# Image patches loaded and turned by token tile, text and image tiles alternating

## The reference

```python
patches = patchify(images, 16)                       # [32, 36, 768]
h_img = einsum('bnd,ed->bne', patches, W_proj) + b_proj + pos_emb
h_txt = take(weights, positions(x_txt), axis=0)      # [32, 32, 256]
h = concatenate([h_img, h_txt], axis=1)              # [32, 68, 256]
h = h + attn(layernorm(h))    # projections dt, x, gate; convolution; state-space scan; output
h = h + ffn(layernorm(h))     # top 2 of 4 experts
```

## Time and profile before

| | us |
|---|---|
| median of 3 runs | 496.74 (496.46 to 499.77) |
| span of the profiled execution | 495.2 |
| its mean granted clock of TensorE | 0.967 |
| TensorE busy | 442.5 (89%) |
| VectorE busy | 330.5 (67%) |
| ScalarE busy | 296.4 (60%) |
| GpSimd busy | 152.2 (31%) |
| stage A, until the first dt projection | 63.7 |

### The profile page before, as it was taken

How to read it: one execution, slowest core, us unless ns; L and a number is a source line. 1 busy time by engine, 2 the same in 40 slices (tenths; PEclk the granted TensorE clock), 3 DMA queues, 4 the chain that set the end, 5 groups by cost and what they waited for, 6 DMA issues and landing times.

```text
span 495.2 us, 9980 instructions
## 1 busy us (share of the span) xinstructions
PE 442.5 (89%) x3149; PEld 363.4 (73%) x3149; DVE 330.5 (67%) x980; ACT 296.4 (60%) x667; POOL 152.2 (31%) x255
## 2 busy tenths in 40 slices
PE   8989989799899999999999798999999999999400
PEld 5769967667778878887777577888878888888300
DVE  6885567678999434335786777866674666666584
ACT  2854359177975465316554354887786777877341
POOL 2000000000000000001243887874778644543322
PEclk9999999799999999999999999999999999999955
DMA  7981089900019942972511222232322333252262
GB/s 178 187 228 56 33 253 322 292 0 2 1 35 259 217 114 58 228 228 81 180 54 52 89 94 77 86 97 66 107 98 76 107 107 110 74 155 69 78 213 82
DMA packets 58734, 59.94 MB, mean 121 GB/s; under 512 B 25368, under 2 KB 51260, under 8 KB 57404
## 3 DMA queue, kind: packets, MB, share of 16 engines
q1 hardware_dynamic: 54236, 48.68, 36.4%
q0 software_dynamic: 3552, 9.74, 5.3%
q10 hardware_dynamic: 896, 0.89, 0.6%
HBM read 34.50 MB, written 24.80 MB: 120 GB/s over the span
## 4 chain that ended last, share of the span: by engine, by line
PE 66%; DVE 12%; issue 7%; ACT 7%; POOL 4%; DMA 2%; SPq 1%; DVEq 0%; POOLq 0%; ACTq 0%
PE bank L1040 14%; PE bank L881 9%; PE bank L433 8%; PE bank L435 8%; PE bank L434 8%; PE bank L955 3%; PE bank L1030 3%; PE bank L901 3%; POOL sorted_x L671 2%; PE bank L1012 2%; ACT U L470 1%; DVE spj L1400 1%; DMA got<-expert_y 1%; PE bank L848 1%; PE bank L947 1%
## 5 line engine op out<-in xcount | busy, mean ns | idle before, releaser
L1040 PE MATMUL bank<-w,hr 128*128 x320 | 76.0, 380 | 1.5 <-DVE ysb L1661 1.5
L1040 PEld LDWEIGHTS bank<-w,hr 128*128 128x128 f32 x320 | 60.1, 190 | 11.7 <-issue 2.7
L644 POOL MEMSET ones<- 2x128 f32 x1 | 0.2, 194 | 212.3 <-PE bank L916 212.3
L1234 ACT ACTIVATE hr<-bank,gsel 128x128 f32<-128x128 f32 x160 | 59.9, 460 | 0.2 <-PE bank L1030 0.2
L719 POOL DMA_INDIRECT expert_y<-ysb,toid x40 | 42.8, 1071 | 51.3 <-DVE ysb L1661 34.7
L881 PE MATMUL bank<-Tb,U 68*32 68x68 f32 x1024 | 45.9, 358 | 0.3 <-issue 0.3
L881 PEld LDWEIGHTS bank<-Tb,U 68*32 68x32 f32 x1024 | 40.6, 139 | 3.6 <-issue 3.1
L1646 DVE BATCH_NORM_STATS2 bsth<-bank 128x6 f32<-128x512 f32 x40 | 27.7, 693 | 20.5 <-PE bank L435 20.2
L671 POOL DMA_INDIRECT sorted_x<-x2s,slot x34 | 33.8, 994 | 15.3 <-issue 9.2
L1226 ACT ACTIVATE hn<-bank,nmrh,rsh 128x512 f32<-128x512 f32 x40 | 31.1, 777 | 10.0 <-DVE nmrh L1655 8.1
L433 PE MATMUL bank<-w_hi,bT_hi 128*128 x80 | 35.0, 438 | 0.1
(11 more groups left out here) (297 smaller groups left out, 1153.3 us busy)
## 6 DMA issues: line engine op xcount, KB each, us to landing
Tb<-ssm_kernels SPq DMA_DIRECT2D x16, 680.0 KB, 7.5
sorted_x<-zpad SPq DMA_DIRECT2D x6, 1419.0 KB, 13.6
xg<-sorted_x SPq DMA_DIRECT2D x40, 129.0 KB, 2.1
got<-expert_y SPq DMA_DIRECT2D x17, 256.0 KB, 3.6
XI<-in_x_dram SPq DMA_DIRECT2D x12, 288.0 KB, 5.6
h0r<-h_spill SPq DMA_DIRECT2D x17, 128.0 KB, 2.1
out_dram<-acc SPq DMA_DIRECT2D x17, 128.0 KB
w1raw<-in_L_ffn_w_dram SPq DMA_DIRECT2D x4, 512.0 KB, 15.9
```

The costliest lines, as they stand in the source:

```text
L1040: mm = pe.matmul(bank[6][:, 0:D], hr[:, i % 3, c, :], w2[:, bass.ds(expert[i], 1), c, :].rearrange("p o n -> p (o n)"), start=(c == 0), st ...
L1234: last = act.activation(hr[:, i % 3, c, :], bank[3 + i % 2][:, c * P:(c + 1) * P], ACT.Relu, scale=gsel[:, i, 0, c:c + 1], bias=gsel[:, i, ...
```

## The change

The images are loaded by token: for each of the 36 positions one load of 32 partitions (the batch) with the 16 pieces of 192 bytes, into the rows of its tile in XI. Four loads make a tile, so all patches of a tile can be turned in two ring steps of three 128x128 transposes, 18 steps in all in place of 24, and an image tile waits only for its own two. Landings are counted in groups: tile 0, tiles 1 and 2, 3 and 4, 5 and 6, 7 and 8. TILE_ORDER alternates text and image tiles and ends with image tile 8. Two img steps stand in every second step, one image tile ahead; vec moves from the ring's start to step 4, and the six weight steps to steps 5, 7, 9, 11, 15 and 16. The filling matmul before each img step is gone. SP issues tok, tabl, the 36 image loads and only then vec_rows. The stores of h0 are in groups of four tiles in the order of their making, and the reading of h0 back follows that. BLOCK_ORDER becomes [0, 3, 4, 1, 2]. The number of bytes moved and the arithmetic of each tile are the same.

The diff, cut to its core:

```diff
@@ -248,7 +246,7 @@
 
 
         x = ins["x"]
-        img = x.rearrange("(g b) (hp py) w c -> g (b hp) py (w c)", g=2, py=PS)
+        img = x.rearrange("b (hp py) (wp px) c -> hp wp b py (px c)", py=PS, px=PS)
         w_dram = [ins[n].rearrange("(c p) d -> p c d", p=P) for n in ("L0_attn_W_dt", "L0_attn_W_x", "L0_attn_W_g")]
 
         def rows(name):
@@ -275,32 +273,43 @@
 
 
 
-        TILE_ORDER = list(range(NTI, NT)) + list(range(NTI))
-        BLOCK_ORDER = [3, 4, 0, 1, 2]
-
-        H0_OUT = [(0, NH0), (NH0, NH0 + 3), (NH0 + 3, NH0 + 6), (NH0 + 6, NT)]
+        TILE_ORDER = [t for n in range(NH0) for t in (NTI + n, n)] + [NTI - 1]
+        BLOCK_ORDER = [0, 3, 4, 1, 2]
+
+        H0_OUT = [(m, min(m + NH0 // 2, NT)) for m in range(0, NT, NH0 // 2)]
 
         def ready_tiles(nb):
 
             t0, t1 = BLOCKS[nb][0] // P, (BLOCKS[nb][0] + BLOCKS[nb][1]) // P
             return 1 + max(TILE_ORDER.index(t) for t in range(t0, t1))
 
-        PREP = [("pos", 0), ("pos", 1), ("vec",)] + [("wp", c) for c in range(0, CK, 2)]
-        IMAGES = [("img", half, g, wp) for g in range(2) for wp in range(HP) for half in range(2)]
+        PREP = [("pos", 0), ("pos", 1)] + [("wp", c) for c in range(0, CK, 2)]
         WEIGHTS = [("w", w, dc) for w in range(3) for dc in range(DC)]
-        A_RING = PREP + IMAGES + WEIGHTS
-        LAST_IMAGES = (len(PREP) + len(IMAGES) - 2, len(PREP) + len(IMAGES) - 1)
-
-        A_STEPS = [("ring", q) for q in range(len(PREP))]
-        ahead = list(range(len(PREP), len(A_RING)))
+        image = lambda i: [("img", i, half) for half in range(2)]
+
+
+        A_RING = PREP + image(0)
+        A_STEPS = [("ring", q) for q in range(len(A_RING))]
+
+        def ring(steps):
+            for step in steps:
+                A_STEPS.append(("ring", len(A_RING)))
+                A_RING.append(step)
+
+        WEIGHTS_AT = [5, 7, 9, 11, 15, 16]
         for k in range(NT + 3):
             A_STEPS += [(f"a{s + 1}", TILE_ORDER[k - s]) for s in (3, 2, 1, 0) if 0 <= k - s < NT]
-            count = 3 if k < NH0 else 1
-            A_STEPS += [("ring", q) for q in ahead[:count]]
-            ahead = ahead[count:]
+            if k % 2 == 0 and k // 2 + 1 < NTI:
+                ring(image(k // 2 + 1))
+            if k == 4:
+                ring([("vec",)])
+            if k in WEIGHTS_AT:
+                ring([WEIGHTS[WEIGHTS_AT.index(k)]])
             if k in (NT, NT + 1):
                 A_STEPS.append(("dt", k - NT))
-        assert not ahead
+        assert all(step in A_RING for step in WEIGHTS + image(NTI - 1))
+        landing = lambda i: (i + 1) // 2
+        images_to = lambda q: sum(step[0] == "img" for step in A_RING[:q + 1])
 
 
         FB = [list(range(i, min(i + 2, NT))) for i in range(0, NT, 2)]
@@ -426,7 +435,7 @@
         def h0_out(eng):
 
             for n in range(len(H0_OUT)):
-                eng.wait_ge(sem(f"h0_stored{n}"), 32 if n == len(H0_OUT) - 1 else 16)
+                eng.wait_ge(sem(f"h0_stored{n}"), 16)
 
         def split3(pe, out_ap, a_hi, a_lo, b_hi, b_lo, start, stop):
 
@@ -443,18 +452,17 @@
             act.activation(spt[:, q % 4, 0:w], spt[:, q % 4, 0:w], ACT.Ln, bias=onec[:]).then_inc(sem("dt_ln"), 1)
 
         def patches(ps):
-            return ps[:, 0:KT * ROWS].rearrange("p (k b hp) -> p k hp b", k=KT, hp=HP)
-
-        def patches_hi(half, g, wp):
-            return pT_hi[:].rearrange("p c (hp wp) b -> p c hp wp b", wp=HP)[
-                :, half * KT:(half + 1) * KT, :, wp, g * GB:(g + 1) * GB]
+            return ps[:, 0:KT * P].rearrange("p (k n) -> p k n", k=KT)
+
+        def patches_hi(i, half):
+            return pT_hi[:].rearrange("p c t b -> p c (t b)")[:, half * KT:(half + 1) * KT, i * P:(i + 1) * P]
 
         def lo_chunk(c):
             return pT_lo[0][:, c, 0:LI * B] if c < KT else pT_lo1[:, c - KT].rearrange("p t b -> p (t b)")
 
-        def patches_lo(half, g, wp):
+        def patches_lo(i, half):
             a = pT_lo[0][:, 0:KT, 0:LI * B] if half == 0 else pT_lo1[:].rearrange("p c t b -> p c (t b)")
-            return a.rearrange("p c (hp wp b) -> p c hp wp b", hp=HP, wp=HP)[:, :, :, wp, g * GB:(g + 1) * GB]
+            return a[:, :, i * P:(i + 1) * P]
 
         def turned(eng, step, who):
 
@@ -477,33 +485,25 @@
         @block.sync
         def _(sp):
             sp.dma_start(tok[:], ins["x_txt"]).then_inc(sem("tok_in"), 16)
+            sp.dma_start(tabl[:], ins["L0_txt_weights"][0:LT + 2, :]).then_inc(sem("table_in"), 16)
+            for i in range(NTI):
+                for n in range(TPT):
+                    t = TPT * i + n
+                    sp.dma_start(XI[n * B:(n + 1) * B, i].rearrange("b (y k) -> b y k", k=PWC),
+                                 img[t // HP, t % HP]).then_inc(sem(f"img_in{landing(i)}"), 16)
             at_row = 0
             for n in VECS:
                 a = rows(n)
                 sp.dma_start(vec_rows[at_row:at_row + a.shape[0], :], a).then_inc(sem("vecs_in"), 16)
                 at_row += a.shape[0]
-            sp.dma_start(tabl[:], ins["L0_txt_weights"][0:LT + 2, :]).then_inc(sem("table_in"), 16)
-            for g in range(2):
-                for wp in range(HP):
-                    sp.dma_start(XI[:, g, wp].rearrange("p (y k) -> p y k", k=PWC),
-                                 img[g][:, :, wp * PWC:(wp + 1) * PWC]).then_inc(sem(f"img_in{g}{wp // 2}"), 16)
             for w in range(3):
                 sp.dma_start(Wr[w][:], w_dram[w]).then_inc(sem(f"w_in{w}"), 16)
 
             for n, (m0, m1) in enumerate(H0_OUT):
                 sp.wait_ge(sem("h0_copied"), m1)
-                t0 = TILE_ORDER[m0]
-                if m0 % NH0 + m1 - m0 <= NH0:
-                    sp.dma_start(h0d[t0:t0 + m1 - m0].rearrange("t p d -> p t d"),
-                                 h0s[:, m0 % NH0:m0 % NH0 + m1 - m0, :]).then_inc(sem(f"h0_stored{n}"), 16)
-                else:
-
-                    cut = NH0 - m0 % NH0
-                    sp.dma_start(h0d[t0:t0 + cut].rearrange("t p d -> p t d"),
-                                 h0s[:, m0 % NH0:, :]).then_inc(sem(f"h0_stored{n}"), 16)
-                    sp.dma_start(h0d[t0 + cut:t0 + m1 - m0].rearrange("t p d -> p t d"),
-                                 h0s[:, 0:m1 - m0 - cut, :]).then_inc(sem(f"h0_stored{n}"), 16)
-                if n == 0:
+                sp.dma_start(h0d[m0:m1].rearrange("m p d -> p m d"),
+                             h0s[:, m0 % NH0:m0 % NH0 + m1 - m0, :]).then_inc(sem(f"h0_stored{n}"), 16)
+                if n == 1:
                     for k in range(2):
                         sp.dma_start(bcs[:, k], state(("L0_attn_B_ssm", "L0_attn_C_ssm")[k])).then_inc(sem("small_in"), 16)
                     sp.dma_start(cw[:], ins["L0_attn_conv_w"].rearrange("(c p) o k -> p c (o k)", p=P)).then_inc(sem("small_in"), 16)
@@ -557,7 +557,7 @@
                 if kind == "h0in":
                     if i >= 4:
                         sp.wait_ge(sem("h1"), i - 3)
-                    sp.dma_start(h0r[:, i % 4, :], h0d[i]).then_inc(sem(f"h0_back{i % 4}"), 16)
+                    sp.dma_start(h0r[:, i % 4, :], h0d[TILE_ORDER.index(i)]).then_inc(sem(f"h0_back{i % 4}"), 16)
                     if i == 3:
                         for t, name in ((ong_b, "L0_ffn_on_g"), (onb_b, "L0_ffn_on_b")):
                             sp.dma_start(t[:], ins[name].partition_broadcast(P)).then_inc(sem("w2_in"), 16)
@@ -755,8 +755,6 @@
                     ps = bank[q % 4]
                     if kind == "wp":
                         warm(ps, 2)
-                    elif kind == "img":
-                        warm(ps, 1)
                     if kind == "vec":
                         pe.wait_ge(sem("vecs_in"), 16 * len(VECS))
                         mm = pe.transpose(ps[:, 0:NV], vec_rows[0:NV, :], ident[0:NV, 0:NV])
@@ -779,12 +777,11 @@
                         for j in range(HC):
                             mm = pe.transpose(ps[:, j * P:(j + 1) * P], Wr[w][:, j, dc * P:(dc + 1) * P], ident[:])
                     else:
-                        half, g, wp = rest
-                        pe.wait_ge(sem(f"img_in{g}{wp // 2}"), 32)
+                        i, half = rest
+                        pe.wait_ge(sem(f"img_in{landing(i)}"), 16 * TPT * min(2, landing(i) + 1))
                         for kk in range(KT):
                             c0 = (half * KT + kk) * P
-                            mm = pe.transpose(ps[:, kk * ROWS:(kk + 1) * ROWS], XI[:, g, wp, c0:c0 + P],
-                                              ident[0:ROWS, 0:ROWS])
+                            mm = pe.transpose(ps[:, kk * P:(kk + 1) * P], XI[:, i, c0:c0 + P], ident[:])
                     mm.then_inc(sem("a_ps"), 1)
                 elif step[0] == "a1":
                     i = step[1]
@@ -800,7 +797,7 @@
                         mm = pe.matmul(ps, at_i, tabl_lo[:], start=False, stop=True)
                     else:
```

(14 more changed lines are left out.)

2 lines of the change are left out of this document (1 added, 1 removed).

## The result

| | before | after |
|---|---|---|
| median of the runs, us | 497.53 (495.67 to 500.0, 8 runs) | 501.5 (499.69 to 503.24, 8 runs) |
| ratio of the times, 95% interval | 1 | 1.0081 (1.0059 to 1.0102) |
| span of the profiled execution, us | 495.2 | 498.0 (its time 499.69) |
| mean granted clock there | 0.967 | 0.962 (other runs 0.953 to 0.959) |

What follows compares the result with a forecast made beforehand. VectorE was taken to bound 12 to 34 us and TensorE 34 to 63; mixing them gains 3.0, less 0.6 at the stage's end, 0.5 for vectors and 0 for blocks: 1.9, so 494.8 us, range 489.5 to 501.

Steps and rivals of the forecast that it cites:

- The start: First ring steps: first image tile at 14.0 us, step 3 at 19.4 and not 17.9.
- The step of the table load: ScalarE, behind the copy of tile 0: loading the square-root table takes 1.28 us; TensorE stands still 1.5 before step 3.
- The loads: SP's queue: 36 image loads at 0.5 us make 18; vectors land at 24.5, making TensorE wait about 0.5 in step 4.
- upper bound: Image loads: 0.14 us per boundary between loads, 5 us for 36; vectors come at 27.5, a wait of 3.7.
- rival 3: Image loads late, vectors and first weights at 27.5 or later, clock perhaps lost: 3 to 5 us, 498.5; 13%.
- The wait inside a pair: Text steps wait for VectorE's xs: 1.97 us, 2.64 after weights; image steps 2.95 or 3.39; pairs 4.92 or 6.03.
- rival 1: Text and image pairs: VectorE reaches xs sooner, pairs take TensorE's own 4.40 and 4.84 us, giving 489.5; 15%.
- The 0.6 given back by the late weight step: End of the image stage: last weight step in step 16, so later xs come 2.64 us after the start, not 1.97.
- The block order: dt projections: q = 8 at 97.6 us, q = 12 at 103.1; between 0.7 gained and 0.6 lost, taken as 0.
- rival 2: Text steps without filling matmuls: clock falls to 1.2 GHz, some 2.2 us a fall; repeated falls 10%, one (497) 12%.
- the price list: Clock falls at image tiles between 17 and 60 us: some 2.2 us each, three falls make 501.4.
- the 1.6 us that I had called safe: Patch and image stage: no expected standstill over 1.6 us, less than half the 3.65 idle in which the clock fell.

Runs made afterwards that it cites:

- g3: e4 with ScalarE's square-root table loaded early, behind the patch copies of step 0: 497.91 us, ratio 1.0001 to the kernel before.
- e2: Changed kernel with the eight vector loads behind the twelve image loads of tiles 0 to 2: 501.38 us, ratio 1.0077 to the kernel before.
- e3: Changed kernel with the old block order (3, 4, 0, 1, 2): 500.13 us, ratio 1.0057 to the kernel before.
- e4: Changed kernel with the vector loads first and the old block order: 497.41 us, ratio 0.9994 to the kernel before.
- e1: Changed kernel with the eight vector loads ahead of the 36 image loads again: 498.75 us, ratio 1.0021 to the kernel before.
- g2: e4 with weight steps in 7, 9, 11, 13, 15 and 16, none in step 5: 496.52 us, ratio 0.9976 to the kernel before.
- g4: Changed kernel with the 18 filling matmuls put back ahead of the patch steps: 501.55 us, ratio 1.0096 to the kernel before.
- j2: Changed kernel with 35 instead of 20 filling matmuls, ahead of dt projection q = 4: 506.05 us, ratio 1.0147 to the kernel before.
- k1: Changed kernel with 13 filling matmuls directly ahead of dt projection q = 8: 503.09 us, ratio 1.0100 to the kernel before.
- g1: e4 with the 18 filling matmuls put back ahead of the patch steps: 497.66 us, ratio 1.0011 to the kernel before.
- h1: g2 and g3 together (vectors first, old block order, weights from step 7, early table): 494.24 us, ratio 0.9944 to the kernel before.
- h2: h1 with the 18 filling matmuls ahead of the patch steps: 494.71 us, ratio 0.9944 to the kernel before.
- j1: Changed kernel with eleven filling matmuls in step 4 ahead of the wait for the vectors: 501.0 us, ratio 1.0059 to the kernel before.
- k2: h1 with 15 filling matmuls directly ahead of dt projection q = 8: 490.74 us, ratio 0.9856 to the kernel before.
- j4: h1 with 35 filling matmuls ahead of dt projection q = 4: 496.94 us, ratio 0.9984 to the kernel before.
- i1: Kernel before with its 12 image loads cut into 36 of 32 partitions each: 503.75 us, ratio 1.0118 to the uncut kernel.

## Why the prediction was wrong

The sum went from -1.9 to +2.8 on the profiles, and to 4.0 in the medians. Term by term:

- **The start: right chain, missed load.** Step 3 came at 20.86, expected 19.4. The images were put 2.8 us earlier "beside the patch weights on ScalarE's queue", whose transfer I priced, but not the small loads behind it there: bpb and araw now come late, and VectorE is 1.2 us behind. Vectors first gives 0.4 to 0.8 of it back. The step of the table load was right: with the table early, step 3 comes 1.5 us sooner (g3). The late start isn't a loss of its own, though. Step 4 waited for the vectors in any case; with step 3 on time it would have waited 4.1 us and not 2.6 (an estimate from their landing at 28.0).
- **The loads: this step failed.** "I take 0.5: 36 x 0.5 = 18": they took 21.97 us. Of the 4.0 that were missing, 35 loads at 0.54 make 1.4, and the one load of 3.11 makes 2.6. For running "beside the patch weights on ScalarE's queue" I had put nothing into the value that I took, only into its bounds. Where the start is as before, a load takes 0.55 to 0.59 on average. The vectors came at 28.0, beyond even my upper bound of 27.5, whose 0.14 a boundary was close to the 0.12 measured; I had dropped it for the nearer-looking 0.50 of a weight load. The wait was 2.61 us, not 0.5. (The 0.5 doesn't follow from my own times either: vectors at 24.5 and TensorE at 23.8 make 0.7.) I had named this as rival 3 (3 to 5 us, 498.5, 13%) with "the idle TensorE may lose the clock too". And I priced vectors and weights apart, where they are one queue: e2 shows that a cure for the one is paid at the other.
- **The wait inside a pair: right.** Text steps 1.96 and 2.63, image steps 2.95 and 3.33 to 3.39, against 1.97, 2.64, 2.95, 3.39. From the start of step 5 to that of step 17 it took 35.5 us (28.25 to 63.76), expected 35.8. So rival 1 didn't occur. The 0.6 given back by the late weight step was 0.67 (step 18 at 66.39 after 63.76, before 65.07 after 63.11).
- **The block order: partly right.** q = 8 was put at 97.6 on the times of before, idle 3.1; it came at 98.88, which less the shift of 1.25 is 97.63, idle 3.17. What I missed is the second pause (0.73) ahead of q = 10, and that the half clock would reach beyond q = 12. On the times of before, q = 12 started at 103.86, not at the 103.1 that I expected; before it was 103.84. "Between -0.7 and +0.6 I take 0" was 1.1 in the profiles, and 1.3 to 1.4 in the medians of e3 and e4. The five traces with the new order and no filler in it have stretches of 52.7 to 54.0, the ten with the old order and none 51.0 to 52.3.
- **The clock: the mechanism of rival 2 exists, its cause was another.** No text step lost the clock by itself, so the price list "image tiles between 17 and 60" didn't apply. It falls around the waits for the root and for loads: the traces of e1, e2, e3, g2, g3, g4, j2 and k1 have such a fall between 20 and 37 us, those of the changed kernel, e4, g1, h1, h2, j1 and k2 don't. j4 has one at 14.6, behind a wait of only 1.04 us for XI, and there image tile 0 took 1.4 us longer than in h1; that is less than the 1.6 us that I had called safe. What a fall adds to the steps behind is 0.4 us (e2) to 2.4 (e3). That the changed kernel's other runs have it too is argued from their mean clocks, and j1 supports it weakly. The Trainium skill's sentence on transposes (TensorE: Matmul & The Clock Gate, Part 4) foretold no loss here: the text steps without fillers ran at 1.00 wherever no long wait stood ahead; whether transposes would have brought a lost clock back, no run shows.

The working of the profile is: -1.9 forecast, +1.5 start, +2.0 vectors, -0.3 steps, +0.1 give-back, +1.1 order, and 0.5 behind adt, well within the 2.9 by which that part differs between traces, in all 3.0 against 2.8 measured. The start and the vectors, 3.5 together, are one cause: by when the vectors landed. The further 1.2 between profile and median is what the clock probably takes.

## What to carry to other kernels

When many loads share a queue, price the queue as one: work out when the last load needed by each early step lands, take the cost of each further load from what full queues show (0.12 us a cut here), add what running beside another queue costs (the stream of 36 took 2.1 us more in the changed kernel than in e1), and test a gain ahead of such a point against it, since it is given back there (g3) until the point is moved (h1). Alternating light and heavy tiles isn't shown to be a gain by itself: with the loads, the weight steps and the old block order put right it is level with the kernel before within the spread (g2, 0.9976, interval up to 1.0002). With the table loaded early it is 0.6% faster, and with filling matmuls right ahead of the one long wait 1.4%, but the kernel before was never run with these two, and with its own fall of 6.8 us it might gain from the second as well. Filling matmuls belong directly ahead of the wait: the same fifteen, four projections earlier, pushed everything back by 3.4 us. Even there they need not pay: k1 filled its first wait and lost the clock behind a later one of 1.38 us.

## What the runs showed of the hardware

- The granted clock fell to 1.2 GHz within a wait of 2.6 us (e3, at 26.9), and just behind waits of 2.0 us (e1 and g2, at 20.9), 1.4 us (k1, at 106.5) and 1.04 us (j4, at 14.6). In other executions with waits of 2.0 and 2.6 us it didn't (changed kernel, e4). The falls seen lasted about 3.4, 6.8 or 10.2 us. I had argued that less than half of 3.65 us of idle time was safe.
- A load of 512 pieces of 192 bytes costs 0.55 to 0.61 us on average in a full queue, whether it reaches 32 partitions or, with 480 to 576 pieces, 96; but the 32-partition cut of i1 took 0.69.
- One load of the stream held SP for 2.3 to 3.2 us in the seven traces where the images start at 1.6, and for at most 0.9 to 1.8 us in the nine where they start at 4.4.
